# One masked add fewer in an attention layer: the decayed product is accumulated in PSUM onto the turned softmax weights

## The chip, the cores and the metric

One core of one Trainium2 chip runs the whole program. The metric is the device time of one execution in microseconds (us), and less is better. The engines are TensorE (PE, with its weight loads as PEld), VectorE (DVE), ScalarE (ACT), GpSimd (POOL) and SyncE (SP, which issues the DMAs). They run their own instruction streams and meet at semaphores.

## The reference, cut to what matters

A layer on x of shape 4 x 512 x 256: attention with 16 query heads and 4 key/value heads of width 128, then a mixture of eight experts, with a layer norm behind each. Each head's output is the mean of two attentions over the same values: an ordinary causal softmax attention on rotated q and k, and a gated linear attention (a state that decays, with softmax features of q and k).

```python
def step(S, inp):
    q_t, k_t, v_t, g_t = inp
    S = S * jnp.exp(g_t)[..., None] + k_t[..., None] * v_t[..., None, :]
    o_t = jnp.einsum('bhk,bhkv->bhv', q_t, S)
    return (S, o_t)
...
scores = jnp.where(causal[None, None], scores, jnp.finfo(scores.dtype).min)
attn = jax.nn.softmax(scores, axis=-1)
y = jnp.einsum('bhqk,bkhd->bqhd', attn, sv)
o = 0.5 * y + 0.5 * o_gla
o = o.reshape(b, n, H * D).astype(hidden_states.dtype)
return o @ Wo
```

In chunks of 128 tokens the linear attention is a product of decayed features inside the chunk, masked to the causal half, plus a part that comes through the carried state.

## The kernel before, in words

The attention goes through 16 groups g (4 batches x 4 key/value heads), each with C = 4 chunks c of 128 tokens, so through 64 steps. A step handles the 4 query heads of its group at once, 128 x 512. Each engine has its own `step(g, c)`, and the order of the calls in it, written by hand, is the order on that engine. Groups 4 to 6 (1 to 6 on VectorE) run in a hardware loop, the others are written out. A step on TensorE, with the lines of the profile:

- `score` (L504, L513): the causal mask of the diagonal block is written into the PSUM tile S by small bf16 products, and the scores of chunk c against chunks 0 to c are accumulated onto it, c + 1 blocks wide. Two heads at a time are announced (`s_sc`).
- `gla_matrix` (L522): the decayed product kdT x qdT, 128 x 512, into the PSUM tile OA. At c = 0 it stands within the projection, as a pair of products, since it must wait until OA was read (`s_oTl`).
- `gate_sums` (L474, L475): the sums of the log gates of chunk c + 1 into MS.
- `project` (L461): q, k and v of chunk c + 2, in 12 products.
- a wait for `s_gc`, since VectorE must have read MS, then `output` (L533): Wo on the output of the chunk before, 12 products into the same MS. In some steps of the last 8 groups, work of the router (`logits`, `prefix`) stands between the wait and `output`.
- `turn_weights` (L542): 4(c + 1) transposes of the normalised weights pr into S, which wait for `s_pn`, the second `normalise` of the step.
- `turn` (L485, L489, L493, L494): ten transposes for chunk c + 1.
- `gather` (L553, L560, L564): the state U and the c + 1 blocks of the weights wT times the values V, into OA; the diagonal block comes last.

VectorE takes the row maxima (`score_max`, L965, twice a step), then in `mask_gla` (L972) multiplies the product in OA by the 0/1 matrix `keep` into the SBUF tile am (at c = 0 this stands behind both `normalise`), then `normalise` (L995 a reciprocal, L999 the product into pr; two heads each), `clamp_gates` (L1008, reads MS and announces `s_gc`; behind the first `normalise` at c = 0, 2, 3, ahead of it at c = 1), `add_output` (L1031), `prepare` (L1040), and `add_gla` (L1048): wT of the diagonal = the turned block of S plus am. ScalarE takes the exponentials between maxima and `normalise` (`exps`, L750: four, each with a read of its running sum behind it), then `exp_gates`, copies (`weights_out` L809, `q_out` L816, `qd_out` L823), and the features of chunk c + 2 (L788).

Behind the attention, TensorE runs 46 tiles of the experts.

Of the kernel before, what the change touches and what calls it, by code (L numbers as in the profile page):

```python
# [37 lines left out]
P128 = 128  # L38
# [42 lines left out]
def layer_kernel(nc, x_rows, x_cols, wqkv, wo_in, wgu, wdn, gate, rope_cos, rope_sin, cmat, cmask, slot_x, slot_y, out):  # L81
    with ExitStack() as ctx:
# [360 lines left out]
        def _(pe):  # L443
# [74 lines left out]
            def gla_matrix(g, c):  # L518
                u = C * g + c
                later(pe, s_oTl, u)  # L520
                pe.wait_ge(s_qdT, u + 1)
                pe.matmul(OA[:, :], kdT[:, :], qdT[:, c % 2, :], start=True, stop=True).then_inc(s_at, 1)  # L522
# [13 lines left out]
            def turn_weights(g, c):  # L536

                u = C * g + c
                pe.wait_ge(s_pn, 2 * (u + 1))
                for j in range(c + 1):  # L540
                    for h in range(GQ):
                        last = pe.transpose(S[:, j, h * 128:(h + 1) * 128], pr[:, h, j * 128:(j + 1) * 128], ident)  # L542
                    last.then_inc(s_pt, 1)

            def gather(g, c, has_next, k=None):

                u = C * g + c
                pe.wait_ge(s_am, u + 1)
# [44 lines left out]
            def step(g, c, first=False, last=False, k=None):  # L593
                n1, n2 = not (last and c >= 3), not (last and c >= 2)
                score(g, c)
                if c:
                    gla_matrix(g, c)
                if n1 and c != 1:
                    gate_sums(g, c + 1)
                if n2:  # L600
# [3 lines left out]
                    if c == 0:  # L604

                        project(g, c + 2, lambda: gla_matrix(g, c), at=2)
                    elif c == 1:

                        project(g, c + 2, lambda: gate_sums(g, c + 1), at=4)
                    else:  # L610
                        project(g, c + 2)
# [16 lines left out]
                turn_weights(g, c)  # L628
                if k in TURN_AT:
                    pe.wait_ge(s_am, C * g + c + 1)  # L630
# [319 lines left out]
        def _(dve):  # L950
# [17 lines left out]
            def mask_gla(g, c):  # L968

                u = C * g + c  # L970
                dve.wait_ge(s_at, u + 1)
                nc.vector.tensor_tensor(exp_view(am[:, :]), exp_view(OA[:, :]),  # L972
                                        keep.rearrange("p (o t) -> p o t", o=1).to_broadcast([P128, GQ, P128]),
                                        ALU.mult).then_inc(s_am, 1)

# [66 lines left out]
            def add_gla(g, c):  # L1042

                u = C * g + c
                dve.wait_ge(s_pt, 10 * g + tri(c) + c + 1)
                dve.wait_ge(s_am, u + 1)
                later(dve, s_o, u)
                nc.vector.tensor_tensor(wT[:, c, :], S[:, c, :], am[:, :], ALU.add).then_inc(s_wtd, 1)  # L1048
# [178 lines left out]
            def step(g, c, first=False, last=False, k=None):  # L1227
# [11 lines left out]
                if c:  # L1239
                    mask_gla(g, c)  # L1240
# [6 lines left out]
                if c == 0:  # L1247
                    mask_gla(g, c)
# [378 lines left out]
```

## Time and profile before

| | us |
|---|---|
| median of 3 runs | 990.01 |
| lowest and highest | 987.09, 993.39 |
| the profiled execution, its own time | 990.93 |
| its span, first to last instruction | 989.0 |

The profile is of one execution. Times within it are counted from the start of its span; 1.9 us lie outside. Its mean granted TensorE clock was 0.979 of full speed. Busy time is that of an engine's instructions; an engine's share is busy time over the span. The attention takes the span from about 26 us (first `score`) to 833 us, and its steps of equal c look alike: from `score` to the next `score` 8.80, 11.4, 13.3 and 15.3 us for c = 0 to 3.

### The profile page before, as it was taken

The page shows a single profiled execution, that of the slowest core. Times are in us where ns is not written, and L with a number is a line of the kernel's source. Part 1 is how long each engine was busy: PE and PEld are TensorE (multiplying, and loading weights), DVE is VectorE, ACT ScalarE, POOL GpSimd, SP SyncE. Part 2 cuts the span into 40 slices and gives each one's busy share as a digit, 9 for nine tenths or more (in the row PEclk, how much of TensorE's full clock was granted, in tenths as well). Part 3 has the DMA queues.
Part 4 walks back from the last instruction along what each step waited for, and adds up shares of the span by engine and source line. Part 5 has one row for each costly group of instructions (what it writes and reads, how often), then busy time and mean ns, then how long its engine had stood idle before and what let it go on. Part 6 is the DMA issues. An engine that isn't in the chain of part 4 may idle for free.

```text
span 989.0 us, 18166 instructions
## 1 busy us (share of the span) xinstructions
PE 924.6 (93%) x5332; PEld 720.6 (73%) x5332; DVE 643.2 (65%) x1483; ACT 661.8 (67%) x2139; POOL 620.6 (63%) x612
## 2 busy tenths in 40 slices
PE   3899999999999999999999999999999989999870
PEld 2767787878777777878778787877777766777650
DVE  4676767676767676767676969676887664321164
ACT  4777777777777777777777777776667664455442
POOL 6658775767565657677767667776658880230374
PEclk9899999999999999999999999999999999999995
DMA  7101100000000000700000000010102121343444
GB/s 247 33 17 33 39 1 1 6 12 6 1 0 0 0 0 7 256 7 1 1 2 1 1 7 6 1 62 2 62 1 78 38 84 42 96 134 102 139 139 148
DMA packets 35648, 44.88 MB, mean 45 GB/s; under 512 B 3568, under 2 KB 29552, under 8 KB 35440
## 3 DMA queue, kind: packets, MB, share of 16 engines
q1 hardware_dynamic: 32496, 35.50, 11.3%
q0 software_dynamic: 3072, 8.39, 2.7%
q8 instruction: 41, 0.67, 0.3%
q14 instruction: 39, 0.32, 0.1%
HBM read 25.52 MB, written 18.35 MB: 44 GB/s over the span
## 4 chain that ended last, share of the span: by engine, by line
PE 84%; ACT 5%; DVE 5%; issue 3%; POOL 1%; another core or an unknown queue 1%; DMA 0%; POOLq 0%; DVEq 0%; ACTq 0%; SPq 0%
PE OA L560 13%; PE PR L461 13%; PE S L513 11%; PE MS L533 9%; PE S L542 7%; PE OA L522 5%; PE S L659 5%; PE OA L676 4%; PE OA L553 4%; PE PR L489 3%; PE PR L485 3%; ACT eqk L788 2%; PE MS L474 1%; PE S L504 1%; PE MS L564 1%
## 5 line engine op out<-in xcount | busy, mean ns | idle before, releaser
L1439 POOL TENSOR_TENSOR qd<-eqk,eg 128x512 f32<-128x512 f32 x63 | 74.8, 1187 | 165.4 <-issue 156.5
L560 PE MATMUL OA<-wT,V 128*128 128x512 f32 x320 | 148.4, 594 | 0.0
L750 ACT ACTIVATE S<-S,nm 128x128 f32<-128x128 f32 (+3 forms) x256 | 126.8, 495 | 25.8 <-DVE nm L965 22.5
L788 ACT ACTIVATE eqk<-qkv,nmx 128x128 f32<-128x128 f32 x320 | 124.3, 396 | 6.9 <-DVE nmx L1040 6.4
L965 DVE TENSOR_REDUCE nm<-S 128x2 f32<-128x256 f32 (+3 forms) x128 | 102.0, 817 | 28.0 <-PE S L513 24.8
L1427 POOL TENSOR_TENSOR eqk<-eqk,rse 128x640 f32<-128x640 f32 x63 | 79.9, 1267 | 52.7 <-DVE rse L1083 28.0
L560 PEld LDWEIGHTS OA<-wT,V 128*128 128x128 f32 x320 | 59.5, 190 | 69.4 <-issue 68.9
L999 DVE TENSOR_TENSOR pr<-S,rl 128x256 f32<-128x256 f32 (+3 forms) x128 | 105.5, 825 | 5.3 <-DVE rl L995 0.3
L1416 POOL TENSOR_TENSOR rp<-qkv,cos 128x640 f32<-128x640 f32 x64 | 99.5, 1554 | 7.2 <-ACT qkv L778 7.0
L1419 POOL TENSOR_TENSOR rp<-rp,rt 128x640 f32<-128x640 f32 x64 | 99.5, 1554 | 5.0
L1416 POOL TENSOR_TENSOR rt<-qkv,sin 128x640 f32<-128x640 f32 x64 | 99.1, 1548 | 0.0
L809 ACT COPY wT<-S 128x512 f32<-128x512 f32 x96 | 51.9, 593 | 53.7 <-PE S L542 53.7
L542 PE MATMUL S<-cm,pr 128*128 128x128 f32 x640 | 82.4, 277 | 3.2 <-DVE pr L999 3.2
L461 PE MATMUL PR<-w_hi,ring_hi 128*128 128x512 f32 (+2 forms) x256 | 77.9, 386 | 7.9 <-DVE w_lo L1333 6.9
L533 PE MATMUL MS<-wo_hi,oT_hi 128*128 128x256 f32 (+1 forms) x256 | 76.1, 297 | 3.8 <-DVE gc L1008 3.2
L542 PEld LDWEIGHTS S<-cm,pr 128*128 128x128 f32 x640 | 73.1, 143 | 3.9 <-DVE pr L999 3.9
L461 PE MATMUL PR<-w_hi,ring_lo 128*128 128x512 f32 (+2 forms) x256 | 73.9, 370 | 0.0
L533 PE MATMUL MS<-wo_lo,oT_hi 128*128 128x256 f32 (+1 forms) x256 | 72.4, 283 | 0.0
L533 PE MATMUL MS<-wo_hi,oT_lo 128*128 128x256 f32 (+1 forms) x256 | 72.4, 283 | 0.0
L461 PE MATMUL PR<-w_lo,ring_hi 128*128 128x512 f32 (+2 forms) x256 | 68.9, 351 | 0.0
L513 PE MATMUL S<-KT_hi,rq_hi 128*128 128x256 f32 (+2 forms) x192 | 68.6, 357 | 0.0
L1299 DVE TENSOR_TENSOR rp<-qd,S 128x176 f32<-128x176 f32 x46 | 15.5, 338 | 80.8 <-ACT qd L875 70.5
(164 smaller groups left out, 2495.9 us busy)
## 6 DMA issues: line engine op xcount, KB each, us to landing
qkv<-slot_x SPq DMA_DIRECT2D x46, 128.0 KB
slot_y<-eqk SPq DMA_DIRECT2D x46, 128.0 KB
gu_w<-in_wgu SPq DMA_DIRECT2D x8, 352.0 KB, 3.6
slot_x<-zero SPq DMA_DIRECT2D x2, 1280.0 KB, 7.3
stage<-in_wqkv SPq DMA_DIRECT2D x6, 384.0 KB, 3.3
xraw<-in_x_cols SPq DMA_DIRECT2D x16, 128.0 KB, 2.3
acc<-in_x_rows SPq DMA_DIRECT2D x1, 2048.0 KB, 11.5
dn_w<-in_wdn SPq DMA_DIRECT2D x8, 256.0 KB, 4.2
```

The source lines that it names most:

```text
L461: last = pe.matmul(PR[:, a:b], x[:, cc, k, :], wq_cols(w, kv, k, a, b), start=(i == 0), stop=(i == len(steps) - 1))
L513: last = pe.matmul(S[:, h, 0:n], q[:, h * 128:(h + 1) * 128], k[:, 0:n], start=False, stop=(i == len(steps) - 1), skip_group_check=True)
L533: last = pe.matmul(MS[:, 0:HID], o[:, h * 128:(h + 1) * 128], r, start=(i == 0), stop=(i == len(steps) - 1))
L542: last = pe.transpose(S[:, j, h * 128:(h + 1) * 128], pr[:, h, j * 128:(j + 1) * 128], ident)
L560: last = pe.matmul(OA[:, :], V[:, j, :], wT[:, j, :], start=(c == 0 and j == 0), stop=(j == c))
L750: nc.scalar.activation(S[:, h, 0:n], S[:, h, 0:n], ACT.Exp, bias=nm[:, h:h + 1], scale=1.0, accum_out=ls[:, h:h + 1]).then_inc(s_exp, 1)
L788: last = nc.scalar.activation(eqk[:, par, h * 128:(h + 1) * 128], qkv[:, c % C, h * 128:(h + 1) * 128], ACT.Exp, bias=nmx[:, h:h + 1], sca ...
L965: nc.vector.tensor_reduce(nm[:, 2 * pair:2 * pair + 2], S[:, 2 * pair:2 * pair + 2, 0:n], AX_X, ALU.max, negate=True).then_inc(s_nm, 1)
L999: nc.vector.tensor_tensor(pr[:, h, 0:n], S[:, h, 0:n], rl[:, h].rearrange("p (h o) -> p h o", o=1) .to_broadcast([P128, 2, n]), ALU.mult). ...
L1416: nc.gpsimd.tensor_tensor(to.rearrange("p (h w d) -> p h w d", w=2, d=64), src, tab, ALU.mult).then_inc(s_rt, 1)
L1419: nc.gpsimd.tensor_tensor(rp[:, c % 2, :], rp[:, c % 2, :], rt[:, :], ALU.add).then_inc(s_rp, 1)
L1427: nc.gpsimd.tensor_tensor(e, e, rse[:, par, :].rearrange("p (h o) -> p h o", o=1) .to_broadcast([P128, GQ + 1, 128]), ALU.mult).then_inc(s ...
```

## The change

The decayed product gets no tile of its own. `gla_matrix` now stands behind `turn_weights` and accumulates (start=False) onto the four turned blocks of the diagonal in S. For this only the first of the four transposes of a bank clears it. One multiplication by `keep` in `add_gla` masks the sum and moves it to wT; the turned softmax weights are already 0 outside the causal half. `mask_gla`, its 64 instructions and its semaphore `s_am` are gone, and so is the wait of `gla_matrix` for OA; at c = 0 the projection is no longer cut by it.

```diff
             def gla_matrix(g, c):
                 u = C * g + c
-                later(pe, s_oTl, u)
                 pe.wait_ge(s_qdT, u + 1)
-                pe.matmul(OA[:, :], kdT[:, :], qdT[:, c % 2, :], start=True, stop=True).then_inc(s_at, 1)
+                pe.matmul(S[:, c, :], kdT[:, :], qdT[:, c % 2, :], start=False, stop=True, skip_group_check=True).then_inc(s_at, 1)
...
-                        last = pe.transpose(S[:, j, h * 128:(h + 1) * 128], pr[:, h, j * 128:(j + 1) * 128], ident)
+                        last = pe.matmul(S[:, j, h * 128:(h + 1) * 128], pr[:, h, j * 128:(j + 1) * 128], ident, start=(h == 0),
+                                         stop=(j < c), is_transpose=True, skip_group_check=True)
...
             def gather(g, c, has_next, k=None):
 
                 u = C * g + c
-                pe.wait_ge(s_am, u + 1)
...
                 score(g, c)
-                if c:
-                    gla_matrix(g, c)
...
-                    if c == 0:
-
-                        project(g, c + 2, lambda: gla_matrix(g, c), at=2)
-                    elif c == 1:
+                    if c == 1:
...
                 turn_weights(g, c)
+                gla_matrix(g, c)
                 if k in TURN_AT:
-                    pe.wait_ge(s_am, C * g + c + 1)
                     turn_tokens(TURN_AT[k], TURN_AT[k] + 1, OA)
...
-            def mask_gla(g, c):
...
             def add_gla(g, c):
 
                 u = C * g + c
-                dve.wait_ge(s_pt, 10 * g + tri(c) + c + 1)
-                dve.wait_ge(s_am, u + 1)
+                dve.wait_ge(s_at, u + 1)
                 later(dve, s_o, u)
-                nc.vector.tensor_tensor(wT[:, c, :], S[:, c, :], am[:, :], ALU.add).then_inc(s_wtd, 1)
+                nc.vector.tensor_tensor(exp_view(wT[:, c, :]), exp_view(S[:, c, :]),
+                                        keep.rearrange("p (o t) -> p o t", o=1).to_broadcast([P128, GQ, P128]),
+                                        ALU.mult).then_inc(s_wtd, 1)
...
                 score_max(g, c, 1)
                 if c == 1:
                     feature_sums(g, c + 1)
-                if c:
-                    mask_gla(g, c)
                 if n1 and c == 1:
                     clamp_gates(g, c + 1)
                 normalise(g, c, 0)
                 if n1 and c != 1:
                     clamp_gates(g, c + 1)
                 normalise(g, c, 1)
-                if c == 0:
-                    mask_gla(g, c)
```

The rows below are built instructions with the semaphores that each waits for. Line numbers of the changed kernel are smaller by one on TensorE (L521 is `gla_matrix`, L532 `output`, L541 `turn_weights`) and by some 14 on VectorE.

TensorE before, the end of `score` in a step c = 3 (group 0) and what follows it:

```order
L513 MATMUL S<-KT_hi,rq_hi 128x512
L513 MATMUL S<-KT_lo,rq_hi 128x512
L513 MATMUL S<-KT_hi,rq_lo 128x512
L522 MATMUL OA<-qdT,kdT 128x512 [waits s_qdT,s_oTl]
L474 MATMUL MS<-gl,cm 128x128 [waits s_kvr,s_kT,s_gl]
L475 MATMUL MS<-cm,gl 128x2
L461 MATMUL PR<-w_hi,ring_hi 128x512 [waits s_rql,s_rqT,s_qdT,s_cp,s_xls]
```

Between here and `output`, the product L522 has gone. TensorE after, in the same step from the last product of `output` to `gather`:

```order
L532 MATMUL MS<-wo_hi,oT_lo 128x256
L541 MATMUL S<-cm,pr 128x128 [waits s_pn]
L541 MATMUL S<-cm,pr 128x128 x15
L521 MATMUL S<-qdT,kdT 128x512 [waits s_qdT]
L485 MATMUL PR<-cm,rp 128x128 [waits s_cp,s_rp]
L485 MATMUL PR<-cm,rp 128x128 x3
L489 MATMUL PR<-cm,qd 128x128 [waits s_qd]
L489 MATMUL PR<-cm,qd 128x128 x3
L493 MATMUL MS<-cm,rp 128x128 [waits s_acc,s_gc]
L494 MATMUL MS<-cm,qd 128x128
L552 MATMUL OA<-qdT,U 128x512 [waits s_U]
```

The product now stands between the transposes of the weights and those for the next chunk, in the same number of instructions as before. VectorE before, in the same step, from the maxima to `add_gla`:

```order
L965 TENSOR_REDUCE nm<-S 128x2 [waits s_exp,s_sc] x2
L972 TENSOR_TENSOR am<-OA,cm 128x512 [waits s_at]
L995 RECIPROCAL rl<-ls 128x2 [waits s_exp]
L999 TENSOR_TENSOR pr<-S,rl 128x1024 [waits s_pt,s_rl]
L1008 TENSOR_SCALAR gc<-MS 128x130 [waits s_eg,s_g]
L995 RECIPROCAL rl<-ls 128x2 [waits s_exp]
L999 TENSOR_TENSOR pr<-S,rl 128x1024 [waits s_pt,s_rl]
L1031 SCALAR_TENSOR_TENSOR acc<-MS,acc 128x256 [waits s_op]
L1040 TENSOR_REDUCE nmx<-qkv 128x5 [waits s_eq,s_cp]
L1048 TENSOR_TENSOR wT<-S,am 128x512 [waits s_o,s_am,s_pt]
```

The masking L972 stands between the maxima and the first reciprocal. VectorE after, the same stretch:

```order
L959 TENSOR_REDUCE nm<-S 128x2 [waits s_exp,s_sc] x2
L981 RECIPROCAL rl<-ls 128x2 [waits s_exp]
L985 TENSOR_TENSOR pr<-S,rl 128x1024 [waits s_pt,s_rl]
L994 TENSOR_SCALAR gc<-MS 128x130 [waits s_eg,s_g]
L981 RECIPROCAL rl<-ls 128x2 [waits s_exp]
L985 TENSOR_TENSOR pr<-S,rl 128x1024 [waits s_pt,s_rl]
L1017 SCALAR_TENSOR_TENSOR acc<-MS,acc 128x256 [waits s_op]
L1026 TENSOR_REDUCE nmx<-qkv 128x5 [waits s_eq,s_cp]
L1033 TENSOR_TENSOR wT<-S,cm 128x512 [waits s_o,s_at]
```

The masking has gone from ahead of the reciprocal, and `add_gla` waits for the product (`s_at`) instead of the transposes.

## Rows read from the trace of the kernel before

**Rows 1.** The page: busy time of each engine, with its share and instructions.

```profile
PE 924.6 (93%) x5332; PEld 720.6 (73%) x5332; DVE 643.2 (65%) x1483; ACT 661.8 (67%) x2139; POOL 620.6 (63%) x612
```

**Rows 2.** Waits by engine: who was waited for, us in total, times, longest.

```profile
ACT rq_hi L816 <- PE PR L485: 26.4, 40, 2.0
...
PE MS L533 <- DVE gc L1008: 3.2, 4, 2.0
PE MS L493 <- DVE acc L1031: 2.9, 2, 1.7
...
PE PR L489 <- POOL qd L1443: 2.0, 1, 2.0
```

**Rows 3.** Groups of instructions by line: the masking. Busy us, mean ns, idle before.

```profile
L972 DVE TENSOR_TENSOR am<-OA,cm 128x512 f32<-128x512 f32 x64 | 43.0, 673 | 1.4 <-PE OA L522 1.4
```

**Rows 4.** Timeline, all engines, one step c = 3: start, us, instruction.

```profile
413.11 1.02 PE L522 MATMUL OA<-qdT,kdT 128*128 128x512 f32 x2
...
413.96 0.38 PE L474 MATMUL MS<-gl,cm 128*128 128x128 f32 x2
...
414.45 0.68 DVE L972 TENSOR_TENSOR am<-OA,cm 128x512 f32<-128x512 f32 x1
414.45 0.20 ACT L750 ACTIVATION_READ_ACCUMULATOR S<-S,nm 128x1 f32 x1
...
415.04 0.15 DVE L995 RECIPROCAL rl<-ls 128x2 f32<-128x2 f32 x1
...
415.23 1.23 DVE L999 TENSOR_TENSOR pr<-S,rl 128x1024 f32<-128x1024 f32 x1
...
416.37 0.28 DVE L1008 TENSOR_SCALAR gc<-MS 128x130 f32<-128x130 f32 x1
...
416.71 0.39 PE L533 MATMUL MS<-wo_hi,oT_hi 128*128 128x256 f32 x1
416.76 1.22 DVE L999 TENSOR_TENSOR pr<-S,rl 128x1024 f32<-128x1024 f32 x1
...
418.24 1.03 PE L542 MATMUL S<-cm,pr 128*128 128x128 f32 x8
```

**Rows 5.** Timeline, all engines, one step c = 2.

```profile
400.49 0.68 DVE L972 TENSOR_TENSOR am<-OA,cm 128x512 f32<-128x512 f32 x1
400.78 0.20 ACT L750 ACTIVATION_READ_ACCUMULATOR S<-S,nm 128x1 f32 x1
401.09 0.15 DVE L995 RECIPROCAL rl<-ls 128x2 f32<-128x2 f32 x1
...
402.15 0.28 DVE L1008 TENSOR_SCALAR gc<-MS 128x130 f32<-128x130 f32 x1
...
402.56 0.32 PE L533 MATMUL MS<-wo_hi,oT_hi 128*128 128x256 f32 x1
...
404.02 1.15 PE L542 MATMUL S<-cm,pr 128*128 128x128 f32 x9
```

**Rows 6.** Timeline, all engines, one step c = 1.

```profile
439.52 0.21 ACT L750 ACTIVATION_READ_ACCUMULATOR S<-S,nm 128x1 f32 x1
439.84 0.15 DVE L995 RECIPROCAL rl<-ls 128x2 f32<-128x2 f32 x1
440.03 0.69 DVE L999 TENSOR_TENSOR pr<-S,rl 128x512 f32<-128x512 f32 x1
...
440.86 0.81 PE L542 MATMUL S<-cm,pr 128*128 128x128 f32 x6
```

**Rows 7.** Timeline, all engines, one step c = 0.

```profile
428.72 0.42 DVE L999 TENSOR_TENSOR pr<-S,rl 128x256 f32<-128x256 f32 x1
...
431.37 0.60 PE L542 MATMUL S<-cm,pr 128*128 128x128 f32 x4
```

**Rows 8.** Stretches behind the two waits of 2.0 us: busy times, PEclk, DMA.

```profile
799.10:803.00 3.90, 3.90 (x19) 2.46 (x20) 1.47 (x5) 3.15 (x14) 3.82 (x3) 1.00 0.00 0
808.30:811.00 2.70, 2.67 (x12) 2.68 (x13) 1.00 (x2) 0.51 (x2) 2.68 (x4) 0.50 0.14 49
```

More of the change, by code:

```diff
@@ L966, in score_max @@
                                         negate=True).then_inc(s_nm, 1)
-            def mask_gla(g, c):
[L970 to L974, printed above, removed]
             def update_state(g, c):
```

## The prediction

> **What bounds the kernel now.** I read the page first: the reader is to see that TensorE is busy for 924.6 of 989.0 us, while no other engine passes 67% [rows 1]. Then TensorE's waits: in the whole attention a handful, each row a few us [rows 2]. So in the 64 steps TensorE hardly waits for anyone, and VectorE's time as such is worth nothing: what counts is the order on TensorE, and how late each of its two gates in a step comes against its arrival. The gates are `output` (L533), which needs VectorE's `clamp_gates` (L1008), and `turn_weights` (L542), which needs the second `normalise` (L999). So the third view is the timeline of one step of each c, to be read as pairs: when the gate's instruction ends, and when TensorE's starts [rows 4 to 7]. At c = 3, `clamp_gates` ends at 416.37 + 0.28 = 416.65 and `output` starts at 416.71 [rows 4]: 0.06 us is what the semaphore takes, and TensorE was waiting there. That 0.06 is my measure of "no cover left" below.
>
> **The work.** TensorE loses no instruction; the one product a step stays. It takes 413.96 - 413.11 = 0.85 us [rows 4]. VectorE loses the masking, 64 x 673 ns = 43.0 us [rows 3]; `add_gla` becomes the same form as the masking, an elementwise product over 128x512 with `keep` spread over the heads, so I cost it at the same 0.67 us. All of this runs on an engine with a third of its time free and is worth nothing by itself.
>
> **The move is what costs.** Ahead of the gates, the 0.85 us of the product were cover: TensorE worked on it while maxima, exponentials and `normalise` ran. They now stand behind `turn_weights`. TensorE reaches each gate 0.85 us earlier. If the gate moves as much, nothing is lost; if it doesn't, the rest is a new wait, and the product is paid in full behind it. How far the gate moves hangs on what held the reciprocal (L995) ahead of `normalise`: the masking, or ScalarE's exponentials. The last read of ScalarE's running sum tells.
>
> At c = 3: the reciprocal starts at 415.04, as the masking (414.45 + 0.68) drains; the exponentials' second read ends at 414.45 + 0.20 = 414.65, so without the masking it can start at 414.71 at the earliest [rows 4]. The gate comes 0.33 us earlier, not 0.85. TensorE was already at its bound, so `output` starts 0.33 earlier, and behind `turn_weights` come 0.85: **+0.52 us**. `turn_weights` has cover of its own: `normalise` ends at 416.76 + 1.22 = 417.98 against 418.24, and moves with the rest.
>
> At c = 2: read ends 400.98, the reciprocal started at 401.09, so it gains 0.05. `clamp_gates` ended at 402.43, `output` started at 402.56: cover was 0.07 [rows 5]. New start 402.44, 0.12 earlier, then the product: **+0.73 us**.
>
> At c = 1 `clamp_gates` stands ahead of `normalise` and follows `gate_sums`, so that gate moves with TensorE. The one that binds is `turn_weights`: the last read ends at 439.52 + 0.21 = 439.73 and its reciprocal starts at 439.84, a gain of 0.05; `normalise` ends at 440.72, TensorE came at 440.86, cover 0.08 [rows 6]. 0.13 earlier, then 0.85: **+0.72 us**.
>
> At c = 0 the last `normalise` ends at 428.72 + 0.42 = 429.14, and TensorE comes at 431.37 [rows 7]: cover 2.2 us, more than 0.85. Taking the product out of the middle of the projection only swaps places: **0**.
>
> **The new wait of `add_gla`.** It waits for the product instead of the transposes, 0.85 us later in TensorE's order. Queued behind it on VectorE are k_out and q_low of the next chunk, which wait for `turn` anyway. `turn` (ten transposes, about 1.1 us, an estimate from the eight in 1.03 of [rows 4]) stood behind the transposes and now stands behind the product, so 0.67 us of VectorE still fit under it at c = 0, and at c > 0 the products with U and the older blocks cover it further: cost 0. What of TensorE's is waited for behind `turn` moves with `turn`: `q_out` (L816) on ScalarE waits for TensorE's transposes in 40 of the 48 steps in which it writes rq_hi [rows 2], so ScalarE doesn't start its next features earlier against TensorE, and the pattern repeats in the next step unchanged.
>
> **An operation that the trace lacks** is a product that accumulates onto a bank that transposes just wrote. Lower bound: the 0.85 as it stands. Upper bound: one more semaphore-like delay of 0.06 per step, 64 x 0.06 = 4 us. I take the lower, as both stand on one engine and need no semaphore, and keep the 4 us for the range; nothing there makes it cheaper.
>
> **Sum.** Per group 0.52 + 0.73 + 0.72 = 1.97 us, times 16: 31.5. Three steps c = 1 of the last groups have a wait of their own behind `turn_weights` (two for VectorE's `add_output`, delayed by router work, 2.9 us; one for GpSimd's decay, 2.0 us [rows 2]), which swallows the 0.72: -2.2. Three other steps c = 1 have the router's logits between the gates, which I put at some 0.45 us of further cover: -1.3 (an estimate). Where TensorE waited already (other waits of L533 in [rows 2], 3 in the first groups and the last), the full 0.85 minus nearly nothing is paid: +0.4. Together **+28.4 us**. The profiled execution had 990.93 us, 0.9 above the median of the three runs; its own sum is 1019.3, by the median 1018.4. I say 1019.
>
> **Rivals.** First, **the masking held more than I read**: if the reciprocal moved by the whole masking, 0.60, at each c > 0 (the reads of ScalarE coming earlier too), a step would cost 0.85 - 0.60 and a little less for the cover of 0.07 at c = 1 and 2: 0.18 + 0.18 + 0.25 = 0.61 a group, 10 us, **1001**. Against it: the reads' ends at c = 1 and 2 leave 0.05.
>
> Second, the other side, **not slower**: ScalarE and VectorE enter the step earlier. At c = 1 and 2 maxima and exponentials don't start when the scores are there but when the two engines have finished the step before; with 0.67 us less on VectorE they could start up to 0.7 earlier, and then both gates follow TensorE. Left would be c = 3, where the maxima wait for the scores: 0.52, or 0.25 with the first rival: 4 to 8 us, **995**, within what can be told from no change. It decides at `q_out`: only if ScalarE is late there today does it gain. It waits for TensorE there [rows 2], so I give this little.
>
> Third, **faster**: what TensorE waits for today (8 us in [rows 2]) goes and the new waits don't come: **984**. The gates' times speak against it.
>
> Fourth, **the clock falls**. Behind one wait of 2.0 us the granted clock was 0.50, the 1.2 GHz level, for 2.7 us, behind the other it stayed 1.00 [rows 8]. The new waits are 0.7 us, 45 of them. If each brought such a stretch, at 1.35 us lost, it would be 61 us more: **1080**. Against it: even of the two long waits one left the clock alone.
>
> The Trainium skill (TensorE: Matmul & The Clock Gate, "A second HAM failure mode: psum-queue depth-cycling") says that short, frequent idling between groups of matmuls can make the clock swing between its levels; by that rule the time is this rival's 1080, by the rows it is the forecast's, and the trace has no stretch of regular waits of 0.7 us to decide it.
>
> **How the numbers follow.** Forecast 0.80; masking held more 0.08; not slower 0.05; faster 0.02; clock 0.05. The forecast's own range is 1010 to 1028: the correction terms either way, 4 us for accumulation, and up to half of the 0.5 to 0.7 misread in one of the three steps (16 x 0.3 = 5). Reaching to the first rival it is 1001 to 1028, which leaves about 0.15 out. A change of 1% (10 us) is about what a measurement of this kernel can tell from none. Faster 0.02, within 0.06, slower 0.92.
>
> **What the changed profile would show.** TensorE's waits: `output` <- `clamp_gates` some 16 to 32 times at 0.7 us, `turn_weights` <- `normalise` some 12 times at 0.7; steps of 12.1, 14.0 and 15.8 us at c = 1, 2, 3 where 11.4, 13.3 and 15.3 stood, 8.8 at c = 0 unchanged; VectorE busy 43 us less; TensorE's busy time unchanged. I am wrong if the exponentials start earlier against `score`, if the reciprocal at c = 2 comes more than 0.1 us earlier, if the product takes other than 0.85 us in its new place, or if PEclk shows stretches below 1 in the middle of the attention.

## The result, and the profile after

The changed kernel takes 1024.06 us (median of 4 runs, 1020.52 to 1029.89) against 989.3 for the kernel before (4 runs): a ratio of 1.0349, with the 95% interval 1.0317 to 1.0381. It is slower by 3.5%. The forecast was 1019.0, its range 1001 to 1028. The profiled execution took 1024.67 us, 33.7 more than the one of before (990.93). One run of the kernel before (1291.93 us, in the session of E5 to E8) and one of E8 (1188.02) ran in a slow state, at mean granted clocks of 0.687 and 0.746, and are left out of every ratio.

The page of the changed kernel: the span, the busy line, the granted clock in 40 equal slices of the span (9 is 0.9 or more of full speed), and the chain that ended last by engine.

```profile
span 1022.9 us, 17960 instructions
...
PE 933.8 (91%) x5332; PEld 717.9 (70%) x5332; DVE 610.9 (60%) x1419; ACT 663.1 (65%) x2139; POOL 621.3 (61%) x612
...
PEclk8899999999999999999999999999999999999995
...
PE 59%; ACT 16%; DVE 13%; issue 8%; POOL 1%; another core or an unknown queue 1%; DVEq 0%; DMA 0%; ACTq 0%; POOLq 0%; SPq 0%
```

The chain of the kernel before:

```profile
PE 84%; ACT 5%; DVE 5%; issue 3%; POOL 1%; another core or an unknown queue 1%; DMA 0%; POOLq 0%; DVEq 0%; ACTq 0%; SPq 0%
```

VectorE has 64 instructions and 32 us less than in [rows 1], and the program is 34 us longer. TensorE has the same 5332 instructions. Its share of the chain fell from 84% to 59%, and ScalarE and VectorE took it over: TensorE has begun to wait. For what, the waits say (engine, line waited for, us in total, times, longest).

```profile
DVE wT L1033 <- PE S L521: 62.6, 59, 4.3
ACT rq_hi L810 <- PE PR L485: 60.2, 40, 2.8
...
PE MS L532 <- DVE gc L994: 19.1, 26, 2.8
...
PE S L541 <- DVE pr L985: 10.6, 14, 2.4
```

`output` waited for `clamp_gates` 4 times for 3.2 us before [rows 2]; now it does so 26 times for 19.1 us. `turn_weights` waits for `normalise` 14 times for 10.6 us. Before it did so 3 times for 3.2 us, a row of that trace which [rows 2] leaves out:

```profile
PE S L542 <- DVE pr L999: 3.2, 3, 1.9
```

ScalarE's wait for the transposes of q, 26.4 us in [rows 2], is 60.2: ScalarE has the time that TensorE lost. The first line is the new wait of `add_gla`; it looks the worst and costs nothing, since no row of TensorE's waits names `wT`, the tile that `add_gla` fills (E9, below, tries it at c = 0 alone).

The step's length, from `score` to the next `score`, taken from the same instruction in both traces, tells where the 33.7 us lie:

| | before | after | change, each | sum over the program | forecast |
|---|---|---|---|---|---|
| c = 0 | 8.80 | 8.82 | 0.02 | -1.3 (the first step of group 0: -1.5) | 0 |
| c = 1, groups 2 to 8 and 11 | 11.4 | 12.23 | 0.77 to 0.83; 0.69 in group 7 | | |
| c = 1, groups 0, 1; 9, 10, 12; 13 to 15 | | | 0.56, 1.46; 0.32 to 0.44; -1.13, -0.02, -0.73 | | |
| c = 1, all 16 | | | from -1.13 to 1.46 | +7.5 | 8.0 |
| c = 2, groups 2 to 7 | 13.3 | 14.4 to 14.6 | 1.05 to 1.27 | | |
| c = 2, groups 8 to 12 (some router work) | 13.5 to 13.9 | 14.3 to 14.7 | 0.78 to 0.84 | | |
| c = 2, all 16 | | | from 0.66 to 1.82 | +17.5 | 11.7 |
| c = 3 | 15.3 (up to 15.98 with router work) | 15.80 (up to 16.47); 15.98 in groups 1 to 6 | 0.5; 0.66 to 0.69 in groups 1 to 6 | +8.5 | 8.3 |

Together 32.2 us; the rest (1.5) lies outside these steps. The -1.5 of the very first step is not the change's work: at the program's start the granted clock stood at 0.50 until 33.4 us in the trace of before and until 31.7 in this one, and that step runs from 26 us on.

The timeline of a step c = 3 of the changed kernel, against [rows 4] (start, us, instruction; in brackets the time for which it waited, and for what):

```profile
800.52 0.20 ACT L744 ACTIVATION_READ_ACCUMULATOR S<-S,nm 128x1 f32 x1
800.76 0.17 DVE L981 RECIPROCAL rl<-ls 128x2 f32<-128x2 f32 x1
800.96 1.23 DVE L985 TENSOR_TENSOR pr<-S,rl 128x1024 f32<-128x1024 f32 x1
...
802.10 0.28 DVE L994 TENSOR_SCALAR gc<-MS 128x130 f32<-128x130 f32 x1
...
802.43 0.39 PE L532 MATMUL MS<-wo_hi,oT_hi 128*128 128x256 f32 x1 [0.52 <-DVE gc L994]
...
803.96 1.91 PE L541 MATMUL S<-cm,pr 128*128 128x128 f32 x16
805.70 1.02 PE L521 MATMUL S<-qdT,kdT 128*128 128x512 f32 x2
```

The reciprocal now starts 0.04 us behind the end of ScalarE's read (800.52 + 0.20 against 800.76), where it stood 0.39 behind it in [rows 4]. The gate came that much nearer and no further; TensorE, without the product ahead of it, waits 0.52. The product then stands behind `turn_weights`. And a step c = 2, against [rows 5], with the last products of the projection (L461) ahead of `output`:

```profile
470.77 0.20 ACT L744 ACTIVATION_READ_ACCUMULATOR S<-S,nm 128x1 f32 x1
471.01 0.17 DVE L981 RECIPROCAL rl<-ls 128x2 f32<-128x2 f32 x1 [0.43 <-ACT S L744]
...
471.34 0.52 PE L461 MATMUL PR<-w_hi,ring_lo 128*128 128x512 f32 x2
...
472.08 0.28 DVE L994 TENSOR_SCALAR gc<-MS 128x130 f32<-128x130 f32 x1
...
472.42 0.38 PE L532 MATMUL MS<-wo_hi,oT_hi 128*128 128x256 f32 x1 [0.56 <-DVE gc L994]
472.64 0.28 PE L532 MATMUL MS<-wo_lo,oT_hi 128*128 128x256 f32 x1
...
473.94 1.47 PE L541 MATMUL S<-cm,pr 128*128 128x128 f32 x12
475.25 1.02 PE L521 MATMUL S<-qdT,kdT 128*128 128x512 f32 x2
476.31 0.69 DVE L1033 TENSOR_TENSOR wT<-S,cm 128x512 f32<-128x512 f32 x1 [1.02 <-PE S L521]
```

The same products in the step of before, which [rows 5] leaves out:

```profile
402.21 0.51 PE L461 MATMUL PR<-w_hi,ring_lo 128*128 128x512 f32 x2
```

Two small things are to be seen around this wait. In the step of before, `output` started 0.35 us behind the start of the last part of the projection (402.21 to 402.56); here it is 1.08 (471.34 to 472.42). The start is 0.73 late, although the trace calls only 0.56 of it idle: the end of a matmul is modelled, its tail counts as busy, and a wait hides in the tail. The distance of starts is the measure. And the first product behind a real wait takes 0.22 us until the next starts (472.42 to 472.64), where it was 0.16 before (402.56 to 402.72): 0.06 more. (At c = 0, where the gate has long been open, it is 0.12 in both kernels.)

And a step c = 1, against [rows 6]: here `turn_weights` is the late one, by 0.55 of idle time, and the transposes of the next chunk (L485) start 0.86 behind the product's start (462.01 to 462.87).

```profile
461.08 1.09 PE L541 MATMUL S<-cm,pr 128*128 128x128 f32 x8 [0.55 <-DVE pr L985]
462.01 1.02 PE L521 MATMUL S<-qdT,kdT 128*128 128x512 f32 x2
462.87 0.60 PE L485 MATMUL PR<-cm,rp 128*128 128x128 f32 x4
```

The groups by line and shape show the product in its new place, and `gate_out` (busy us, mean ns of one):

```profile
L521 PE MATMUL S<-qdT,kdT 128*128 128x512 f32 x128 | 66.4, 601 | 0.0
...
L1077 DVE SCALAR_TENSOR_TENSOR gl<-qkv,lnp 128x128 f32<-128x128 f32 x64 | 29.5, 461 | 28.7 <-ACT lnp L795 28.4
```

The product's 128 instructions had a mean of 601 ns before too: accumulating onto freshly turned blocks is not dearer than writing a bank of its own. In 62 of the 64 steps the next instruction starts 0.86 us behind the product's start; the other two ran into a stretch at half clock. The second line, `gate_out`, comes up again in E5.

### The profile page after: what moved, and what is told of

It is laid out like the page before. It is cut to its first block, busy times and chain, and to the rows that moved or that the text cites. A ratio compares the mean times of both kernels' runs of the same rounds, so it can differ in the third digit from the quotient of the medians.

```text
span 1022.9 us, 17960 instructions
## 1 busy us (share of the span) xinstructions
PE 933.8 (91%) x5332; PEld 717.9 (70%) x5332; DVE 610.9 (60%) x1419; ACT 663.1 (65%) x2139; POOL 621.3 (61%) x612
## 3 DMA queue, kind: packets, MB, share of 16 engines
q1 hardware_dynamic: 32496, 35.50, 10.9%
## 4 chain that ended last, share of the span: by engine, by line
PE 59%; ACT 16%; DVE 13%; issue 8%; POOL 1%; another core or an unknown queue 1%; DVEq 0%; DMA 0%; ACTq 0%; POOLq 0%; SPq 0%
PE OA L559 9%; PE MS L532 7%; PE S L541 7%; ACT S L744 6%; PE S L521 5%; ACT eqk L782 5%; PE S L653 5%; PE PR L461 4%; PE S L513 4%; PE OA L670 4%; PE OA L552 3%; DVE nm L959 3%; PE PR L485 3%; PE PR L489 2%; DVE pr L985 2%
## 5 line engine op out<-in xcount | busy, mean ns | idle before, releaser
L532 PE MATMUL MS<-wo_hi,oT_hi 128*128 128x256 f32 (+1 forms) x256 | 76.4, 298 | 19.4 <-DVE gc L994 19.1
L541 PE MATMUL S<-cm,pr 128*128 128x128 f32 x640 | 83.5, 279 | 11.3 <-DVE pr L985 10.6
L541 PEld LDWEIGHTS S<-cm,pr 128*128 128x128 f32 x640 | 72.8, 144 | 14.8 <-DVE pr L985 14.0
L1033 DVE TENSOR_TENSOR wT<-S,cm 128x512 f32<-128x512 f32 x64 | 44.2, 691 | 63.8 <-PE S L521 62.6
L461 PE MATMUL PR<-w_hi,ring_hi 128*128 128x512 f32 (+2 forms) x256 | 71.5, 361 | 7.5 <-DVE w_lo L1316 6.6
L532 PE MATMUL MS<-wo_lo,oT_hi 128*128 128x256 f32 (+1 forms) x256 | 72.4, 283 | 0.0
L532 PE MATMUL MS<-wo_hi,oT_lo 128*128 128x256 f32 (+1 forms) x256 | 72.0, 281 | 0.0
L532 PEld LDWEIGHTS MS<-wo_hi,oT_hi 128*128 128x128 f32 x256 | 48.4, 189 | 29.9 <-DVE gc L994 28.1
L810 ACT CAST rq_hi<-PR 128x512 fp32r<-128x512 f32 x48 | 28.2, 587 | 62.2 <-PE PR L485 60.2
## 6 DMA issues: line engine op xcount, KB each, us to landing
acc<-in_x_rows SPq DMA_DIRECT2D x1, 2048.0 KB, 10.6
```

The source lines that it names most:

```text
L461: last = pe.matmul(PR[:, a:b], x[:, cc, k, :], wq_cols(w, kv, k, a, b), start=(i == 0), stop=(i == len(steps) - 1))
L532: last = pe.matmul(MS[:, 0:HID], o[:, h * 128:(h + 1) * 128], r, start=(i == 0), stop=(i == len(steps) - 1))
L541: last = pe.matmul(S[:, j, h * 128:(h + 1) * 128], pr[:, h, j * 128:(j + 1) * 128], ident, start=(h == 0), stop=(j < c), is_transpose=True ...
```

## The experiments

E9 and E10 were timed in a session in which the kernel before had a median of 992.03 us, E5 to E8 in one with 993.07, the others in one with 989.18; so they are compared by ratios to it. "After" is the changed kernel, 1.0349. Lengths of steps are of the profiled executions. In those, single steps of group 0 and of the last three groups differ by up to 2 us from run to run, partly with the clock: in a part of step c = 2 of group 15 (step 62, counted from 0) the granted clock was 0.50 in the traces of both kernels, before and changed, and 1.00 in those of E5, E6 and E8. So the readings below rest on the steps between.

### E1: the kernel before with the product moved, nothing accumulated

```diff
                 score(g, c)
-                if c:
-                    gla_matrix(g, c)
...
                 turn_weights(g, c)
+                gla_matrix(g, c)
...
-                if c:
-                    mask_gla(g, c)
...
+                mask_gla(g, c)
                 add_gla(g, c)
```

The product still goes into OA, and VectorE still masks it into am, now directly ahead of `add_gla`.

> The kernel before with the move alone: the product still goes to its own PSUM tile and is masked by itself, but it stands behind the transposes of the weights, and VectorE masks it directly ahead of the add. If the lost cover ahead of the two gates is the cause, this must be as slow as the changed kernel, 1024 us, plus some 0.3 us a step c = 0 and 0.1 at the others, where two VectorE operations instead of one now follow the product: 1026 to 1036. If accumulating onto just turned weights in PSUM is itself dear, it must be faster than the changed kernel by that, below 1020. If the rival holds that removing the masking from in front of the reciprocal is what matters, the time follows neither.

Measured: 1040.37 us (1038.96 to 1042.31), ratio 1.0516 [1.0486, 1.0545]: slower than the change itself, by more than I expected. The gates behave as in the changed kernel; its own waits of TensorE are these:

```profile
PE MS L533 <- DVE gc L1004: 17.9, 24, 2.8
PE OA L571 <- DVE am L968: 9.4, 12, 0.8
PE S L542 <- DVE pr L995: 8.4, 13, 1.8
...
PE OA L560 <- DVE wT L1044: 7.4, 13, 0.6
```

The first and third lines are nearly those of the changed kernel (19.1 and 10.6): so the new waits come of the move, without any accumulation. The second and the fourth are what a mask *behind* the product costs, when TensorE has to wait for VectorE to free OA and to fill wT; the accumulation saves these. The steps show it against the changed kernel: +0.61 at c = 0, and +1.0 in the twelve steps (three of them c = 0) in which tokens are turned into OA. At c = 1 most steps are 0.33 shorter than after the change (ScalarE's reads end 0.33 earlier against `score`, behind a step c = 0 in which TensorE was held up), at c = 2 and 3 about 0.1 in groups 1 to 6; in the others without tokens the two are equal at c = 3.

### E2: the changed kernel with the masking kept in its old place

```diff
+                if c:
+                    mask_old(g, c)
                 if n1 and c == 1:
                     clamp_gates(g, c + 1)
                 normalise(g, c, 0)
```

`mask_old` is the instruction of before (48 of the 64), on what OA holds at that time, and `gather` and `turn_tokens` wait for it; its result goes nowhere.

> The changed kernel with the old masking operation left in its old place on VectorE for c > 0 (it now reads the tile of the last output and its result is used by nobody). If ScalarE's exponentials hold the reciprocal, as I read it, the masking costs about 0.05 us at c = 1 and 2 and 0.33 at c = 3: 7 us, 1031. If the masking held it (first rival), each gate comes 0.6 later and the time is near 1024 + 29 = 1053. If VectorE's time is free altogether, 1024.

Measured: 1028.7 us (1025.35 to 1030.36), ratio 1.0391 [1.0358, 1.0424]. That is nearer to 1031 than to the 1053 of the first rival, which falls; the interval overlaps that of the changed kernel, so the time alone can't tell 7 us from nothing. The steps can. Against the changed kernel a step is longer by 0.00 at c = 1, 0.06 at c = 2, 0.27 to 0.38 at c = 3. These are the gains that the removed masking brings: the forecast had read 0.05, 0.05 and 0.33 from the distance between ScalarE's last read and the reciprocal. The 48 maskings, 32 us of VectorE's work (48 x 673 ns), were worth about 5.

### E3: the changed kernel with the product of U and q put where the decayed product had stood

```diff
-                if c:
-                    pe.wait_ge(s_U, 3 * g + c)
-                    pe.matmul(OA[:, :], U[:, :], qdT[:, c % 2, :], start=True, stop=False)
+                if c and k in TURN_AT:
+                    state_part(g, c)
...
+                if c and k not in TURN_AT:
+                    state_part(g, c)
                 if n1:
                     pe.wait_ge(s_gc, C * g + c + 2)
```

The other product of the same size is taken out of `gather` and put ahead of the wait of `output`, as cover (not in nine steps whose router work uses OA).

> The changed kernel with the cover given back by other work: the product with the carried state (0.86 us, c > 0) moves from the head of gather to just ahead of the wait for clamp_gates, except in 9 steps where the router's transposes use the same PSUM tile. If the cover is the cause, 39 of 48 waits of some 0.7 us go: 1024 - 27 = 997, with an error of 4. If the loss sits elsewhere (accumulation, clock, contention between GpSimd and VectorE), most of the 34 us stays: above 1010.

Measured: 1009.07 us (1006.19 to 1012.09), ratio 1.0208 [1.017, 1.0247]. A gain, but 12 us less than expected. Per step against the changed kernel: c = 1 -0.8 and c = 3 -0.5 in most steps in which the product was moved, but c = 2 nothing in groups 1 to 7 and 11, and 0.75 to 0.88 *longer* in groups 8, 9, 10 and 12, where the product was moved in the step before and not in this one. TensorE's waits:

```profile
PE MS L474 <- DVE Ut L980: 13.3, 16, 2.5
PE MS L532 <- DVE gc L1001: 7.0, 13, 1.9
...
PE S L541 <- DVE pr L992: 2.7, 3, 1.5
```

The wait of `output` fell from 26 times to 13, and a new one of 13.3 us stands ahead of `gate_sums`: VectorE's update of the state (Ut), 0.2 to 1.4 us in the c = 2 steps after group 0. In groups 4 to 6 the end of `clamp_gates` at c = 2 moved from 6.07 us behind `score` to 6.9, as far as TensorE's work had moved. So my picture of cover was too simple. At c = 2 maxima and exponentials don't start at `score`: the engines come to them from a chain that `turn` of the step before set off (`q_out`, `qd_out`, the features, the reading of OA, the state). Its length can be read: in group 8 the maxima start 5.89 us behind the first transpose of `turn` in all three traces (441.73 to 447.62 before, 462.87 to 468.76 after the change, 452.92 to 458.81 here), while `score` stood 2.0, 2.0 and 2.86 us ahead of them. Work moved from behind `turn` to before `output` stays in the same stretch between `turn` and the gate and shortens nothing; only at c = 1 and 3, where less or nothing hangs on that chain, does it act as cover.

### E4: the same move in the kernel before

> The same move of the state's product in the kernel before, where cover was still 0.07 us or more at c = 1 and 2 and missing by 0.17 at c = 3. If only missing cover costs, this gains at most 0.2 us in the c = 3 steps, 0 to 3 us: 987 to 990. If the place of this product has a price or a gain of its own, it shows here, and the run before must be corrected by it.

Here the moved product waits for the masking too, which reads OA (`s_am`).

Measured: 989.15 us (986.95 to 991.38), ratio 1.0005 [0.9989, 1.0022]. The zero is not "nothing happened". Against the kernel before, the steps c = 2 are 0.56 to 0.86 us longer in most groups from 2 to 12 (8.4 in sum), those of c = 3 shorter by 0.3 in most groups (2.7 in sum), and five steps c = 1, in groups 0, 1 and 13 to 15, shorter by 3.3 in sum; the others didn't move. TensorE's new wait is at c = 2 alone, `gla_matrix` for OA to be read:

```profile
PE OA L522 <- DVE oT_lo L965: 7.3, 14, 2.3
```

The lengthening fits E3's reading: the moved product had stood between `turn` and the next `score`. With it gone `score` stands 0.86 nearer to `turn`, while the chain from `turn`, of which the reading of OA is a part, takes as long as before.

### E5: the changed kernel, GpSimd held back until `gate_out` is done

In the changed kernel, groups 2 to 7, the gates at c = 2 are 0.4 us later than in groups 8 and on. The cause that the timeline offers lies at the end of the step before (group 4 here):

```profile
259.48 1.55 POOL L1402 TENSOR_TENSOR rp<-rp,rt 128x640 f32<-128x640 f32 x1
260.97 1.27 POOL L1410 TENSOR_TENSOR eqk<-eqk,rse 128x640 f32<-128x640 f32 x1
...
261.43 0.95 DVE L1077 SCALAR_TENSOR_TENSOR gl<-qkv,lnp 128x128 f32<-128x128 f32 x1 [0.70 <-ACT lnp L795]
...
262.17 0.36 POOL L1431 COPY V<-qkv 128x128 f32<-128x128 f32 x1
```

`gate_out` takes 0.29 us where GpSimd is at rest; here it takes 0.95, and ends 0.14 behind GpSimd's `weigh_features` (260.97 + 1.27 = 262.24 against 261.43 + 0.95 = 262.38). It stood beside GpSimd's work in the kernel before as well, but for less: in groups 2 to 7 it took 0.42 to 0.71 there, and 0.83 to 0.95 after the change. The experiment makes `weigh_features` wait for it:

```diff
                 if not (last and c == 3):
+                    pool.wait_ge(s_gl, C * g + c + 2)
                     weigh_features(g, c + 1)
```

> The changed kernel with one wait more on GpSimd: it begins to weigh the features of chunk c + 1 only when VectorE has finished gate_out of that chunk. In the changed kernel gate_out at c = 1 took 0.83 to 0.95 us in groups 1 to 7 (0.29 elsewhere, 0.3 to 0.6 before) while GpSimd weighed features, and VectorE's maxima of c = 2 came 0.4 late. Theory: the two disturb each other, both read SBUF; kept apart, gate_out takes 0.29, clamp_gates at c = 2 comes 0.4 earlier in some 7 groups, and at c = 3 0.15: 3 to 4 us, 1020 to 1021. Rival: the 0.4 has another cause (ScalarE's chain or the order of GpSimd): 1024.

The same place:

```profile
260.06 0.29 DVE L1077 SCALAR_TENSOR_TENSOR gl<-qkv,lnp 128x128 f32<-128x128 f32 x1 [0.69 <-ACT lnp L795]
260.58 1.26 POOL L1410 TENSOR_TENSOR eqk<-eqk,rse 128x640 f32<-128x640 f32 x1 [0.95 <-DVE gl L1077]
```

Measured: 1023.15 us (1021.61 to 1025.16), ratio 1.0316 [1.0289, 1.0343]; between this and 1.0349 the intervals overlap, so the time alone decides nothing. The steps do: `gate_out` is 0.29 in groups 2 and 4 to 6 and their steps c = 2 are 0.31 to 0.39 shorter; in groups 3 and 7, where it still takes 0.81, they didn't move (-0.01 and 0.00). There it stands beside another operation of GpSimd (L1444, 128x256, the low part of the input's split), which the new wait does not hold back. All c = 2 together: -5.6 us, of which 1.5 in group 0, 0.9 in step 54 and 1.7 in step 62. The first and the last are steps in which the granted clock fell to 0.50 for 3.4 us in the trace of the changed kernel (from 55.6 and from 840.6 us) and not in this one; for step 54 I have no cause. Steps c = 3 didn't move (-0.01).

### E6: the changed kernel, `clamp_gates` ahead of the first `normalise` at every c > 0

```diff
-                if n1 and c == 1:
+                if n1 and c:
                     clamp_gates(g, c + 1)
                 normalise(g, c, 0)
-                if n1 and c != 1:
+                if n1 and c == 0:
                     clamp_gates(g, c + 1)
```

> The changed kernel with clamp_gates ahead of the first normalise at c = 2 and 3 too, as it already stands at c = 1. The sums that it reads are ready early now, and VectorE sits idle there for 0.4 us until the exponentials come. The gate of output then is open when TensorE arrives, and only turn_weights waits for the second normalise: at c = 2 some 0.45 us less, at c = 3 some 0.4: 32 x 0.43 = 14 us, 1010. If the new waits are not at these gates (or only shift from one to the other by the full amount), 1024.

```profile
PE S L541 <- DVE pr L985: 17.7, 34, 2.4
...
PE MS L532 <- DVE gc L994: 1.2, 1, 1.2
```

Measured: 1008.25 us (1006.42 to 1009.7), ratio 1.0167 [1.0138, 1.0196]. Expected was 1010 against a kernel before of 989.3, which is 1.021: the direction and place are as expected, the gain is some 18 us instead of 14. `output` no longer waits, but for one step. `turn_weights` does, 34 times instead of 14, for 0.5 us on average: the second gate stands behind the first, and was covered by its wait. Steps c = 2 are 0.53 to 0.62 shorter in groups 1 to 12; c = 3 0.28 to 0.33, and 0.72 to 0.78 in the five steps with router work, which the expectation had not set apart.

### E7: E6 and E3 together

> The changed kernel with both: the state's product ahead of output (1009) and clamp_gates ahead of normalise at c = 2 and 3. If at c = 2 the gate hangs on ScalarE's chain from the transposes of the chunk, not on when the scores start, then the wait at c = 2 is at output and falls by some 0.7 us in the 11 or so steps without router work, at c = 3 by 0.3 to 0.4: 1009 - 12 = 997. It would beat the kernel before only if the waits vanish altogether: below 985.

Measured: 1000.05 us (999.11 to 1002.18), ratio 1.0081 [1.005, 1.0112], which is the 997 expected against 989.3. Against the changed kernel c = 1 gives back 10.9 us, c = 3 11.3, c = 2 only 2.6. What is left of TensorE's new waits:

```profile
PE MS L474 <- DVE Ut L980: 14.4, 16, 2.5
...
PE S L541 <- DVE pr L992: 3.7, 8, 1.5
```

With one product put back as cover and the gates in the better order, the accumulation is still 0.8% behind the kernel before. By steps it is ahead of it at c = 0, 1 and 3 (by 1.5, 3.4 and 2.8 us) and 14.9 us behind at c = 2, where TensorE now waits for the state.

### E8: the kernel before, with the order of `clamp_gates` of E6

> The kernel before with clamp_gates ahead of the first normalise at c = 2 and 3. There output waited 0.17 us at c = 3 and nothing at c = 2, so it can gain 16 x 0.17 = 2.7 us at most: 987 to 989, no difference that can be told. If it gains as much as in the changed kernel, the waits that I blame for the loss are not new.

Measured: 985.68 us (five runs, 982.35 to 986.77), ratio 0.993 [0.9904, 0.9956]: faster than both kernels, and by some 7 us where I had expected 2.7 at most, so the expectation missed. Steps c = 3 are 0.11 to 0.32 shorter, 2.8 us in sum, as expected. What I had put at nothing is the rest: four steps c = 2 (groups 0, 1, 10, 11) are 0.25 to 0.5 shorter, 1.6 in sum. Another 2.4 us of this trace, in the first step and in step 62, go with a clock that rose sooner (at 30.8 instead of 33.4 us) and did not fall in step 62, so they are not to be credited to the order. `output` waits for `clamp_gates` in step 62 alone (0.94 us), and the product still covers what `turn_weights` would wait for:

```profile
PE S L542 <- DVE pr L999: 3.3, 4, 1.7
PE MS L493 <- DVE acc L1031: 3.0, 2, 1.7
```

### E9: the change at c = 0 alone

```diff
                 turn_weights(g, c)
+                if c == 0:
+                    gla_matrix(g, c)
```

At c = 0 the product goes onto S and the masking is gone, as in the change; at c > 0 all is as before.

> The change made at c = 0 alone: there the product is accumulated onto the turned weights behind turn_weights, masked in add_gla; at c > 0 everything stands as before. At c = 0 the cover was 2.2 us, more than the product's 0.85, so if cover is the whole story this costs and gains nothing: 990, within 3. If accumulating in PSUM, the single masked move or the longer wait of add_gla has a price, 16 steps show it: 0.85 a step would be 14 us.

Measured: 991.8 us (12 runs, 987.9 to 996.28), ratio 1.0001 [0.9983, 1.0018]. Where the gate has 2.2 us of cover [rows 7], the accumulation, its transposes with a single clearing one, the masked move and the longer wait of `add_gla` cost nothing that the time shows; they gain nothing either. (The steps c = 0 are within 0.02 but for the first; the steps c = 1 behind them are 0.05 to 0.07 longer in groups 2 to 7 and 0.59 in group 1.)

### E10: E8 and E9 together

> The same, with clamp_gates ahead of the first normalise at c = 2 and 3, which alone made the kernel before faster (0.993 of it). The two should add up: the change at c = 0 is worth nothing, so 0.993 of the kernel before, some 983 to 986. It would be the best of both; below 0.990 would mean that the change at c = 0 has a gain of its own.

Measured: 985.35 us (983.56 to 987.57), ratio 0.9935 [0.9911, 0.9959], the same as E8.

## Why the prediction was right, and where it was short

**The bound and the gates: right.** TensorE's order decides, and the two gates became its waits: 26 of `output`, 14 of `turn_weights`, forecast 16 to 32 and 12. E1 has the move without the accumulation and shows the same waits, E6 takes away the one and uncovers the other. The rows picked for the forecast left out three waits that `turn_weights` had before (3.2 us, two of them at c = 1 of groups 0 and 1), so those two steps were costed like the rest: 0.72 each, measured 0.56 and 1.46.

**The masking's worth: right.** E2 measured 0.00, 0.06 and 0.27 to 0.38 us a step for what had been read as 0.05, 0.05 and 0.33. "The masking held more" would have asked for 0.60 and falls.

**The product's price: right.** The next instruction starts 0.86 us behind it, forecast 0.85; the mean per instruction is 601 ns on both sides, so the upper bound of 4 us for the accumulation fell away. E9 confirms it at c = 0.

**c = 0 and 3: right. c = 1: right in sum, by luck.** The sums are -1.3, +8.5 and +7.5 against 0, 8.3 and 8.0. At c = 1 the ten steps without router work or another wait took 8.3 us where 7.2 were forecast, the three with router work 1.1 instead of 0.8, and the three with another wait behind `turn_weights` came out 1.9 *shorter* where 0 was forecast: two misses that cancel. At c = 3 two parts hide in the sum: 0.5 in groups 0 and 7 on, as forecast from a step of group 7, but 0.66 to 0.69 in groups 1 to 6, which VectorE runs in its hardware loop. Half of that excess was there to be read in the trace of before: in these groups ScalarE's read ends 0.1 later against `score`, so that the masking held the reciprocal by 0.27 to 0.29 and not 0.36 to 0.38. The other half is a new gap of 0.09: from the start of the reciprocal to that of `normalise` it is 0.29 us (280.05 to 280.34) instead of 0.20 (800.76 to 800.96). I had taken this for register instructions in front of a wait that used to be passed early, but the traces speak against it: in E1 the reciprocal starts as early and the gap is 0.20, in E2 it starts as late as before and the gap is 0.27 to 0.28. It comes with the changed program and not with the early start; which instruction stands in it is open.

**c = 2: the term that was mis-sized.** The sum had 0.73 for each of 16 steps, 11.7 us; measured were 17.5, a mean of 1.09. Four things stand in the 5.8 us between. The start of `output` is later by the 0.73 as forecast, but a gate that had been passed and is now waited at costs 0.06 more for its first product, so that the plain case is 0.79: 1.0 us in 16 steps. (At c = 1 the first transpose of `turn_weights` likewise takes 0.17 instead of 0.11 until the next starts; at c = 3 TensorE had waited before, and nothing was added.) In groups 2 to 7 come 0.26 to 0.48 more, 2.4 us in sum. Of this, 0.25 to 0.4 in each is `gate_out`, which the slower pace moves further into GpSimd's operations and which delays the maxima (they start 2.26 to 2.39 behind `score` instead of 2.0). E5 takes that away in groups 2, 4, 5 and 6, has the maxima back at 2.0 and gets 0.31 to 0.39 back in each, which leaves 0.09 above the plain case, the gap of the hardware loop again; in groups 3 and 7, where `gate_out` stayed long, nothing came back. The remainder, 2.3 us, lies in three steps. In group 0 (0.3) the granted clock fell to 0.50 for 3.4 us behind a wait of 1.63 us for the state. In group 1 (1.0) and step 54 (c = 2 of group 13, 1.74 instead of 0.79) the mechanisms are not separated. My line "the pattern repeats in the next step unchanged" was the error: the engines off the bound don't all shift along with TensorE, and the overlaps between them are new ones.

**Busy times: half right.** VectorE's busy line fell by 32 us, not 43. Summed over its groups by shape, VectorE's time went from 706.7 to 663.2 us, and that is the masking's 43. The busy line counts overlapping instructions once, and the masking had overlapped with its neighbours by 7.9 us in sum (as the reciprocal at 415.04 starts ahead of 414.45 + 0.68 in [rows 4]). I should have forecast the line by starts. The other 3 us, overlaps of other instructions that grew smaller, I have not placed. TensorE's line grew by 9 us with the same work; the tails ahead of some 40 waits, of which each leaves about 0.2 uncovered, would make that up, an estimate from the step shown (0.73 late, 0.56 idle).

**The clock: right for the middle of the attention.** The rival of 1080 us asked for a falling clock behind the new waits. Two stretches of the changed kernel, with busy times, clock and DMA: one within step c = 2 of group 0, and all that lies between it and a point in step 62.

```profile
55.70:58.90 3.20, 2.89 (x11) 2.19 (x11) 2.19 (x5) 2.90 (x11) 0.23 (x1) 0.50 0.00 0
59.20:840.50 781.30, 749.56 (x4452) 578.93 (x4451) 512.72 (x1156) 548.46 (x1806) 524.18 (x494) 1.00 0.07 23
```

Through nearly all of the new waits, most of them of 0.5 to 0.75 us, the clock stayed at 1.00, the 2.4 GHz level: TensorE idled for 31.7 of 781.3 us here. So 1080 falls. The first stretch, 3.4 us long at the 1.2 GHz level behind a wait of 1.63 us, is one that the kernel before did not have (it waited 1.43 us in the same step, and its clock stayed at 1.00); it cost at most 1.7 us, an estimate from half of its length. The stretch behind the longest wait, 2.80 us in step 62, was in both kernels: [rows 8] shows 2.7 us of it, its whole length before was 3.4. The rule of the Trainium skill that stood behind the rival (TensorE: Matmul & The Clock Gate, "A second HAM failure mode: psum-queue depth-cycling") is not borne out by waits of this length and spacing.

**"Not slower": fell.** It had the two engines enter the step earlier. At c = 3 the reads end where they did against `score`; the gate that binds came 0.06 earlier against `score` at c = 1 (the second `normalise`) and 0.07 at c = 2 in groups 8, 9 and 12, against 0.05 read, and later than before in groups 2 to 7. What E3 and E4 added is that at c = 2 the two engines enter by the chain from `turn`, a thing that I had only used to dismiss the rival and not to size the term.

## What to carry to other kernels

An instruction taken off an engine with time to spare is worth only what it held up for the bound engine, and that is read from the distance between its follower and the follower's other input: here 0.05 to 0.33 us of each 0.67. What the same edit moves on the bound engine counts in full: work that stood ahead of a wait was its cover, and behind the wait it is paid in full while the wait takes its old place, unless the cover left is larger (2.2 us at c = 0, no cost; 0.07 at c = 2, where 0.79 of 0.86 was paid). Before counting a piece of work as cover, ask from which event the late engine's chain is counted; if that lies ahead of both places, the move shortens nothing.

## What the runs showed of the hardware

A matmul behind a real wait takes 0.06 us longer until the next one starts than the same matmul behind a gate that was passed (0.22 against 0.16 for `output` at c = 2; at c = 3, where it waited in both kernels, 0.23 in both: 416.71 to 416.94 and 802.43 to 802.66). The first transpose of `turn_weights` at c = 1 shows the same: 0.17 behind a wait, 0.11 before. So a wait of TensorE costs a little more than it is long.

A VectorE operation with two inputs in SBUF and no PSUM, 128x128, took 0.29 us alone, 0.88 to 0.95 us while GpSimd ran an operation over 128x640 (groups 2 and 4 to 6) and 0.83 beside one over 128x256 (groups 3 and 7), and ended 0.15 us behind it each time. That agrees with the Trainium skill (GPSIMD Engine Reference, "1. Specifications", the table's line on SBUF interfaces), which says that the two engines contend when VectorE has two SBUF inputs. `normalise` and `clamp_gates`, which read PSUM, took 1.22 and 0.28 to 0.29 us whether GpSimd was at work beside them or not.

A plain fp32 product that accumulates onto four blocks which transposes had just written into the same bank costs what it costs in a cleared bank: 601 ns per instruction in both, and 0.86 us per product until the next instruction starts (1.05 and 1.55 in the two that ran at the 1.2 GHz level for a part).
